# The first batch of an attention kernel gets a plan of its own for its row maxima

## The reference

```python
q = x @ Wq.T + bq
kv = x @ Wkv.T + bkv
dots = jnp.einsum('bhid,bhjd->bhij', q * scale, k)
dots = jnp.where(causal, MASK_VAL, dots)
attn = jax.nn.softmax(dots, axis=-1)
out = jnp.einsum('bhij,bhjd->bhid', attn, v)
...
x = x + 0.5 * _L0_ffn_ref(_layernorm(x, axis=-1), ...)
x = x + _L0_attn_ref(_layernorm(x, axis=-1), ...)
x = x + 0.5 * _L0_ffn_ref(_layernorm(x, axis=-1), ...)
```

## Time and profile before

| what | value |
|---|---|
| median of 3 runs | 1387.4 us |
| the profiled execution: its own time, its span | 1384.99 us, 1383.3 us |
| busy share of PE, DVE, ACT, POOL | 92%, 79%, 68%, 29% |
| first `s` unit, first `st` unit | 34.69 us, 77.57 us |
| start of batch 0's four steps and of batch 1 | 77.57, 113.47, 148.87, 184.77, 220.30 us |
| mean granted PE clock over the span | 0.983 of full speed |

### The profile page before, as it was taken

The page is one execution under the profiler, slowest core; times in us unless marked ns, Lnnn a source line. Parts: engine busy times, 40 slices in busy tenths (PEclk is TensorE's granted clock), DMA queues, the critical chain, the costliest instruction groups (busy, mean ns, idle before and its releaser), DMA issues.

```text
span 1383.3 us, 25088 instructions
## 1 busy us (share of the span) xinstructions
PE 1277.5 (92%) x8693; PEld 600.4 (43%) x8693; DVE 1098.5 (79%) x3527; ACT 941.2 (68%) x1697; POOL 397.7 (29%) x508
## 2 busy tenths in 40 slices
PE   6899999999999999999999999999999999999974
PEld 4433444444454444454444444544444544444332
DVE  6888888778888888878887788887888788779744
ACT  2267776777767677767767677677776677676662
POOL 3223232323223322232323322232232323222111
PEclk9889999999999999999999999999999999999997
DMA  4680333542415443234335424254431354340001
GB/s 134 121 146 16 66 69 59 98 98 51 73 29 99 89 69 70 46 77 89 69 59 100 70 68 72 41 100 89 69 70 32 49 100 70 58 69 32 1 1 33
DMA packets 57832, 95.18 MB, mean 69 GB/s; under 512 B 8352, under 2 KB 51488, under 8 KB 51744
## 3 DMA queue, kind: packets, MB, share of 16 engines
q1 hardware_dynamic: 55664, 92.30, 35.2%
q10 hardware_dynamic: 2032, 1.19, 0.3%
HBM read 59.91 MB, written 33.55 MB: 68 GB/s over the span
## 4 chain that ended last, share of the span: by engine, by line
PE 60%; DVE 16%; ACT 12%; issue 4%; POOL 2%; DVEq 2%; DMA 2%; SPq 1%; POOLq 0%; ACTq 0%
PE o_bank L1300 15%; PE s L1281 13%; PE st L1266 12%; PE misc L1183 6%; ACT probs L841 5%; ACT q_stack L828 5%; DVE s L992 4%; PE misc L1167 4%; PE misc L1175 4%; DVE max_full L996 3%; PE misc L524 2%; DVE stats L491 2%; POOL probs L715 1%; DVEq L1003 1%; PE misc L515 1%
## 5 line engine op out<-in xcount | busy, mean ns | idle before, releaser
L841 ACT ACTIVATE probs<-st 128x512 f32<-128x512 f32 (+1 forms) x1216 | 633.2, 582 | 202.8 <-PE st L1266 112.4
L992 DVE CUSTOM_DVE_ANT_0 s<-s,causal 128x128 f32<-128x128 f32 (+3 forms) x1024 | 494.7, 502 | 144.9 <-PE s L1281 141.7
L1281 PE MATMUL s<-k_stack,q_stack 96*128 96x512 bf16 (+3 forms) x1536 | 494.9, 332 | 25.2 <-DVE max_full L996 9.4
L1266 PE MATMUL st<-q_stack,k_stack 108*128 108x512 bf16 (+3 forms) x1536 | 486.3, 329 | 23.9 <-ACT probs L841 21.6
L996 DVE TENSOR_REDUCE max_full<-s 128x1 f32<-128x512 f32 x512 | 350.1, 684 | 42.8 <-PE s L1281 41.3
L1300 PE MATMUL o_bank<-probs,v_aug 128*17 128x512 f32 (+3 forms) x3072 | 324.8, 495 | 7.8 <-POOL probs L715 6.5
L715 POOL TENSOR_SCALAR_AFFINE_SELECT probs<-probs 128x512 f32<-128x512 f32 x256 | 163.7, 644 | 533.1 <-ACT probs L841 532.8
L1281 PEld LDWEIGHTS s<-k_stack,q_stack 96*128 96x128 bf16 x1536 | 149.9, 98 | 348.0 <-DVE max_diag L992 150.1
L1266 PEld LDWEIGHTS st<-q_stack,k_stack 108*128 108x128 bf16 x1536 | 149.2, 98 | 132.7 <-ACT probs L841 53.3
L727 POOL TENSOR_TENSOR qk<-qk,parts 128x512 f32<-128x512 f32 x64 | 75.1, 1174 | 313.2 <-ACT parts L801 313.2
L992 DVE DVE_READ_ACCUMULATOR2_ANT max_diag<- 128x1 f32 x1024 | 144.4, 141 | 0.0
(11 more groups left out here) (115 smaller groups left out, 892.7 us busy)
## 6 DMA issues: line engine op xcount, KB each, us to landing
part_dram<-parts SPq DMA_DIRECT2D x128, 192.0 KB, 2.8
k_stack<-part_dram SPq DMA_DIRECT2D x186, 128.0 KB, 7.0
q_stack<-part_dram SPq DMA_DIRECT2D x31, 384.0 KB, 5.0
x_all<-x SPq DMA_DIRECT2D x16, 512.0 KB, 11.0
q_stack<-part_dram SPq DMA_DIRECT2D x31, 256.0 KB, 7.3
out<-x_all SPq DMA_DIRECT2D x7, 1024.0 KB, 11.4
q_stack<-part_dram SPq DMA_DIRECT2D x33, 128.0 KB, 8.8
k_stack<-part_dram SPq DMA_DIRECT2D x12, 64.0 KB, 3.0
```

The costliest lines, as they stand in the source:

```text
L841: nc.scalar.activation(probs[:, g % 2, h - part:h + 1, 0:width], st_bank[i % 3][:, 0:share * width] .rearrange("p (h c) -> p h c", c=width ...
L992: nc.vector.tensor_tensor_reduce(out=bank, in0=bank, in1=causal[:, CW - width:CW], scale=1.0, scalar=-BIG, op0=ALU.add, op1=ALU.max, accum ...
L1266: score = nc.tensor.matmul(st_bank[i % 3][:, part * width:(part + 1) * width], k_stack[0:KROWS + MROWS, hg, h, jb * P:(jb + 1) * P], q_sta ...
L1281: nc.tensor.matmul(s_bank[u % 3][:, 0:width], q_stack[0:KROWS, hm, h, ib * P:(ib + 1) * P], k_stack[0:KROWS, hm, h, j0:j0 + width], start= ...
```

## The change

Batch 0 is given another order. The prologue runs only 24 `s` units (`FRONT`) instead of 63, and only the two half projections of group 1 instead of six. Then batch 0 begins. In it the number of `s` units done by each `st` unit follows a broken line, `FRONT_RAMP`: 24 at `st` unit 0, 48 at 12 (two `s` per `st`), 98 at 48, 150 at 96, 202 at 144, and 255 at 192, which is where the kernel before stands too. The four other half projections are put at `st` units 5, 17, 27 and 37 of the first step (`FRONT_QK`), the turns of the maxima at places of their own (`FRONT_MTR`). The turn of group 0's second half of maxima now runs in batch 0, so the first `st` unit of group 4 gets a wait for it. The other batches keep their plan.

```diff
-    "total0": 7, "pro_qk": (4, 14, 26, 35, 44, 53), "pro_before": (6, 16),
+    "total0": 7, "pro_qk": (4, 14), "pro_before": (6, 17),
...
+FRONT = 24
+FRONT_RAMP = ((0, FRONT), (12, NU), (NU, 2 * NU + 2), (2 * NU, 3 * NU + 6), (3 * NU, 4 * NU + 10), (4 * NU, 5 * NU + EARLY))
+FRONT_QK = ((2, 5), (2, 17), (3, 27), (3, 37))
+FRONT_MTR = {(0, 1): 13, (1, 0): 31, (1, 1): NU, (2, 0): NU + 17, (2, 1): NU + 45, (3, 0): 2 * NU + 15,
+             (3, 1): 2 * NU + 42, (4, 0): 3 * NU + 14, (4, 1): 3 * NU + 40}
...
+def maxima_by(t):
+    for (t0, n0), (t1, n1) in zip(FRONT_RAMP, FRONT_RAMP[1:]):
+        if t <= t1:
+            return n0 + (n1 - n0) * (t - t0) // (t1 - t0)
...
+    if hg == 0 and not prev:
+        for i, (hq, u) in enumerate(FRONT_QK):
+            put(u, ("use", "qk", hq, i % 2))
+            put(u + Q2_LAG, ("q2", hq, i % 2))
+            put(u + Q3_LAG, ("q3", hq, i % 2))
...
-            if hg + ahead < NG or nxt:
+            if not prev:
+                plan += [("s",) + unit for unit in front_units.get(NU * hg + HG * g + h, ())]
+            elif hg + ahead < NG or nxt:
                 plan.append(("s", ahead, u % NU))
...
-    for u in range(NU + EARLY):
+    for u in range(FRONT):
...
+                    if b == 0 and hg == 0 and (g, h) == (CT, 0):
+                        eng.wait_ge(sig.misc_free, n("use", 1))
```

More of the change, by code:

```diff
@@ L127, with front_maxima @@
 WARM = (26, 20, 1)
+FRONT = 24
[7 more added lines that the diff above has]
+            return n0 + (n1 - n0) * (t - t0) // (t1 - t0)
+def front_maxima():
+    units, more = {}, {}
+    for t in range(NG * NU):
+        for i in range(maxima_by(t), maxima_by(t + 1)):
+            group, u = divmod(i, NU)
+            units.setdefault(t, []).append((group - t // NU, u))
+            for c in range(2):
+                for k in range(MFIN_PARTS[c]):
+                    first = i + 1 - HALF_UNITS[c]
+                    if first % NU == 0 and 0 <= first // NU <= NG and i >= FRONT:
+                        more.setdefault(t, []).append(("of", first // NU - 1, "mfin", c, k))
+    for (group, c), t in FRONT_MTR.items():
+        more.setdefault(t, []).append(("of", group - 1, "use", "mtr", c))
+    return units, more
 def step_plan(hg, prev, nxt, spec):
+    front_units, front_more = front_maxima() if not prev else (None, {})
     extra, early = {}, {}
@@ L212, in step_plan @@
                     place.setdefault(u - back, []).append(("piece", quarters) + e[1:])
-    if hg < NG - 1 or nxt:
+    if not prev:
+        for u in range(NU):
+            put(u, *front_more.get(NU * hg + u, ()))
+    elif hg < NG - 1 or nxt:
         for c in range(2):
@@ L229, in step_plan @@
             ahead = 1 + u // NU
-            if hg + ahead < NG or nxt:
+            if not prev:
+                plan += [("s",) + unit for unit in front_units.get(NU * hg + HG * g + h, ())]
+            elif hg + ahead < NG or nxt:
                 plan.append(("s", ahead, u % NU))
             plan += early.get(HG * g + h, []) + extra.get(HG * g + h, [])
-    return [(hg,) + e for e in plan]
+    return [e[1:] if e[0] == "of" else (hg,) + e for e in plan]
 def batch_plan(prev, nxt, spec):
```

## The result

The changed kernel is slower: 1402.78 us (median of 4 runs, 1399.39 to 1403.56) against 1385.97 us, ratio 1.0118 (95% interval 1.0104 to 1.0132). Forecast were 3 us less. The profiled execution took 1403.16 us with a span of 1401.4 us.

What follows compares the result with a forecast made beforehand. PE bounds the whole kernel, but DVE is fuller at the front and paces step one. Batch 1 starts at 106.0 + 111.3 = 217.3 us instead of 220.3, 3.0 sooner, giving 1384 us; range 1377 to 1392.

Steps and rivals of the forecast that it cites:

- Part 1: Up to unit 48: batch 0 starts 26 us sooner, at about 51.6 us; unit 48 starts as before, 68.1 to 68.4 us.
- Part 2: `st` units 12 to 48: DVE sets the pace, 36.1 us at 91.5% busy plus 1.5 us stalls; `st` 48 at 106.0 us.
- Part 3: Batch 0's other three steps: they get back 13 units, 4.5 us more, 111.3 us in all.
- A: Batch 0: DVE nearly full, 97% up to `st` 48; 8.5 us gained, about 1379 us; chance 0.22.
- B: Batch 0: the engines wait for each other in today's shares; 1.0 us lost, 1388 us; chance 0.15.
- C: Batch 0: PE's clock at half for 15 of 37 us in the first step; 6 us lost, about 1393 us; chance 0.18.

Runs made afterwards that it cites:

- e2: Changed kernel with 48 instead of 24 `s` units ahead of batch 0, so no `st` unit runs beside units 24 to 47: 1405.9 us.
- e16: e13 with 48 `s` units ahead of batch 0, so no `st` unit runs beside units 24 to 47: 1395.9 us.
- e12: Changed kernel with the products of the four half projections in step one of batch 0 done twice over: 1407.3 us.
- e7: Changed kernel with group 3's two half projections at `st` units 23 and 34 instead of 27 and 37: 1396.2 us.
- e15: Changed kernel with 14 `s` units instead of 6 on `st` units 12 to 16: 1402.9 us.
- e13: Changed kernel with splits one to an `st` unit, turns of steps two and three among narrow units, group 3's projections at `st` units 23 and 34: 1392.5 us.
- e14: e13 with 14 `s` units instead of 6 on `st` units 12 to 16: 1389.5 us.
- e17: e14 with the splits of group 4 again in one run, as in the changed kernel: 1389.0 us.
- e18: e17 with step one's four half projections each run as four single products on four `st` units: 1390.0 us.
- e3: Kernel before without the single filler products between the prologue's `s` units (the two filler blocks stay): 1385.5 us.
- e10: Changed kernel with the turns of steps two to four moved to narrow `st` units and the splits one to an `st` unit: 1396.5 us.
- e11: Kernel before's prologue with the changed kernel's small lead in batch 0, turns moved to narrow `st` units and splits spread: 1393.7 us.
- e4: Changed kernel with a filler product of 256 columns ahead of each `s` product of batch 0: 1412.2 us.

## Why the prediction was wrong

By its own sum, batch 1 was to start at 217.3 us and starts at 236.5: 19.2 us. They lie in three terms.

**Part 1 held in the number.** First `st` at 52.7 us (51.6 predicted), unit 48 at 69.7 (68.4), a late 1.3 us. DVE was busy 15.18 of 16.96 us, as said. The stack landed at 68.8 us (68.07 before), and PE was then still in the `pv` ahead of unit 48, whose 1.5 us the sum had not counted there. Worth of the twelve early `st` units: 3.1 and 3.4 us (e2, e16).

**Part 2 failed by 5.9 us**, in the sentence "DVE sets the pace. At the share which the fullest step of the trace reaches, 91.5%, it takes 36.1 us". It took 43.5 us with DVE at 73%. One error is a plain misreading: a half projection was priced at four products of 0.22 us, but the trace lists each 128x256 product as two records, and four of them take 1.72 us (the block in the profile after: 88.77 us, 1.08 us for half of one). Three of them are 5.2 us of PE time and not 2.6. The other error is the choice of engine: DVE does not set the pace. e12 shows PE's time there at full price (6.0 us for 5.2 in the trace). The waits on `misc`, for which 1.5 us stood, were worth 3.1 us in step one when two of them were removed (e7). And the clock was at half for 7.8 us of the stretch, where the step that the 91.5% came from had 3.5. The row for DVE's 91.5% came from a step that had no projections and the full lead; the share was carried to a step that had three and a quarter of the `st` units fewer.

**Part 3 failed by 12.0 us.** "They get back 13 units" priced units alone, 4.5 us. The places of the turns (`FRONT_MTR`) and the splits in one run stood in the sum at nothing, without a reason: I had read them as moves without a price. The same order at full clock takes 41.8 (e15), 39.9 (e2) and 38.0 us, 119.7 together, so 3.6 of the 12.0 us are the stretches at half in steps two and three. With turns and splits placed as in e13 and e14, the same units take 37.4 and 37.5 us in steps two and three at full clock: 6.8 us are the places. What is left, 1.6 us, is from steps of different runs; no run has all three at once. The best sum in one run with this lead is e14's 114.6 us, 3.3 over the forecast; its step four takes 39.8 us at full clock instead of 38.0, and e17 and e18 take 38.9 with its splits in one run. Why step four loses there is not shown. The lead of 2 units brings a group's last split 2 `st` units ahead of the step's end, its turn to `st` unit 0, where exponentials are 512 wide, and the splits, four or five in a row, hold DVE for 1.2 us (113.80 to 114.96 in the trace) with filled banks behind them. In the kernel before, the turns stand at `st` units 33 and 40, 39 and 42, 14 and 40, 14 and 42 (`PLACE["mtr"]` in the code), and the splits one to a unit.

**Rivals.** A was refuted: nowhere is DVE at 97%. B, "the coupling stays", pointed the right way and was far too cheap (1 us lost). C, the clock, had the nearest number (6 lost) and is a part: 36.7 us at half between 34 us and batch 1 instead of 17.1. Steps of the same order with and without a stretch at half give about 0.25 to 0.45 us for each us at half (last section), so the 19.6 us more are some 5 to 9 us of the 16.8 (an estimate). C's own sign, a mean clock under 0.8 in the first step, didn't come (0.91 in part 2's stretch), and its condition, the removal of fillers, made no difference in the kernel before (e3). The stretches don't follow from the places alone: e10 has none in steps two and three, e17 has 10.2 us in the same two steps with the same order in step two, and e11 6.8. What decides between the two is not shown.

What stays open: with all repairs the stretch from unit 48 to `st` unit 48 takes 40.5 (e13), 41.4 (e14) and 42.7 us (e17), 3 to 5 over the 37.6 predicted. PE's time in the projections is 2.6 us of it. The exposed turn (e14, e15) and the shape of the projections (e18) showed no gain; between the clock, at half for 9 to 16 us of it, and the density of `s` units the runs don't decide.

## What to carry to other kernels

Where two engines share a few banks and neither is full, don't carry the busy share of one step to another; count both engines' added time at full price (PE's filler cost 0.58 us per us in the calmest place here) and take DVE's idle time as PE's, until a row shows the reverse. In a table of places, the small jobs that go with the units (a 1.9 us copy on the engine that also does the exponentials, a row of splits) can cost more than the units: the places of the turns and the spread of the splits were some 7 us in two steps, at the same clock. Before putting a difference down to a change, compare the clock of the two traces: here the same order of work took 37.4 or 40.1 us. Look at how the profile counts a product before multiplying: two records may be one.

## What the runs showed of the hardware

What TensorE's clock at half (1.2 GHz instead of 2.4) costs can be read from steps in which PE, DVE and ACT do the same work in the same order, in different runs:

| step and order | no time at half | 3.4 us at half | 6.8 us at half |
|---|---|---|---|
| two, changed kernel's | 41.8 (e15) | | 43.6 (changed), 44.0 (e2, e7, e12) |
| three, changed kernel's | 39.9 (e2) | | 41.7 (changed, e15), 42.3 (e12), 42.8 (e7) |
| two, turns and splits moved | 37.4 (e13, e14) | 38.9 (e18) | 40.1 (e17) |
| three, turns and splits moved | 37.4 (e13), 37.5 (e14, e18) | 38.9 (e17) | |
| four, e13's | 39.8 (e14) | | 41.8 (e13) |

That is about 0.25 to 0.45 us for each us at half, less than the 0.5 that products lose which follow each other without a gap at both clocks (an estimate from the two levels). Single filler products between the `s` units of the old prologue changed neither the time nor the stretches at half (e3, 17.1 us with and without 35 of them); 231 ahead of the `s` units of batch 0 cut the stretches at half from 36.7 to 19.9 us and cost more than that gave (e4, 9.4 us slower).
